# Gate logits in the attention stage: the tokens held in the array, the sixteen gate columns passing

## The reference, cut to what matters

```python
x = x + tanh(g_xattn) * attention(layernorm(x), ctx)      # 16 heads of 16
xn = layernorm(x)
logits = einsum('bld,ed->ble', xn, gate_weight)           # 8 experts
kth_val = sort(logits.reshape(-1))[expert_k - 1]
gates = logits * (logits >= kth_val)
h = gelu(einsum('bld,ehd->bleh', xn, w1) + b1)
y = einsum('bleh,edh->blde', h, w2) + b2
x = x + tanh(g_ffn) * einsum('blde,ble->bld', y, gates)
```

## Time and profile before

| | |
|---|---|
| three runs | 2002.65, 2004.87, 2005.2 us, median 2004.87 |
| profiled execution | 2004.73 us, of which the span between first and last instruction is 2002.9 |
| granted clock of TensorE, mean | 0.976 |
| busy: PE, PEld, DVE, ACT, POOL | 95%, 68%, 66%, 62%, 7% of the span |
| gate matmuls L887 | 32 |
| pick matmuls L894 | 64 |
| copies L1129, reads L1026 | 8 and 8 |

### The profile page before, as it was taken

One profiled execution on the slowest core, in us unless ns is written; L12 is line 12 of the kernel. 1 busy time (PEld: TensorE's weight loads), 2 busy tenths in 40 slices (PEclk: granted clock), 3 DMA queues, 4 the chain that ended last, 5 costly groups with the idle time before them and its releaser, 6 DMA issues.

```text
span 2002.9 us, 26039 instructions
## 1 busy us (share of the span) xinstructions
PE 1897.7 (95%) x8916; PEld 1357.2 (68%) x8916; DVE 1322.1 (66%) x2331; ACT 1242.3 (62%) x2081; POOL 146.7 (7%) x330
## 2 busy tenths in 40 slices
PE   7889999999968989999999999999999999999998
PEld 5743333333337867788788878878878887887886
DVE  6588888888725787565655665565665566656555
ACT  4447776767743323676676667667666666667664
POOL 4300011101112260000000000000000000000000
PEclk9979999999978999999999999999999999999999
DMA  6933323222110144333323333233422224232221
GB/s 240 329 118 86 83 71 83 71 74 70 49 53 24 74 176 184 122 143 114 106 84 108 148 118 110 85 106 119 149 101 94 106 98 161 97 108 84 106 105 53
DMA packets 97243, 220.81 MB, mean 110 GB/s; under 512 B 31314, under 2 KB 49492, under 8 KB 87892
## 3 DMA queue, kind: packets, MB, share of 16 engines
q1 hardware_dynamic: 97108, 219.12, 31.9%
HBM read 178.57 MB, written 40.24 MB: 109 GB/s over the span
## 4 chain that ended last, share of the span: by engine, by line
PE 61%; DVE 3%; ACT 2%; issue 2%; POOL 0%; ACTq 0%; DVEq 0%; POOLq 0%
PE ps_y L2140 29%; PE ps_h L2087 25%; PE ps_h L2047 4%; PE ps_y L2059 3%; ACT gelu L2294 1%; DVE w_pair L2520 1%; ACT w_pair L2264 1%; DVE early L2528 1%; DVE h_lo L2395 1%; DVE out_T_acc L2471 1%; ACT h_hi L2297 0%; DVE early L2483 0%; DVE h_hi L2391 0%; DVE gated L2464 0%; ACT copy L2304 0%
## 5 line engine op out<-in xcount | busy, mean ns | idle before, releaser
L2395 DVE TENSOR_TENSOR h_lo<-gelu,h_hi 128x512 fp32r<-128x512 f32 x512 | 355.4, 698 | 412.8 <-ACT h_hi L2297 411.7
L2087 PE MATMUL ps_h<-x_hi,w_pair 128*128 128x512 f32 x1568 | 567.3, 395 | 11.3 <-ACT gelu L2294 9.4
L2294 ACT ACTIVATE gelu<-early,b 128x512 f32<-128x512 f32 x336 | 243.2, 724 | 236.1 <-DVE early L2528 228.7
L2087 PEld LDWEIGHTS ps_h<-x_hi,w_pair 128*128 128x128 f32 x1568 | 294.5, 188 | 88.7 <-issue 13.4
L964 DVE TENSOR_REDUCE low<-ps_s 128x1 f32<-128x512 f32 x512 | 322.3, 684 | 35.2 <-PE ps_s L820 31.9
L2297 ACT ACTIVATE h_hi<-gelu 128x512 fp32r<-128x512 f32 x448 | 283.3, 632 | 42.0 <-ACT gelu L2294 0.7
L2087 PE MATMUL ps_h<-x_lo,w_pair 128*128 128x512 f32 x784 | 308.7, 394 | 0.0
L1096 ACT ACTIVATE probs_T<-ps_t 128x512 f32<-128x512 f32 x384 | 207.8, 600 | 105.3 <-PE ps_t L830 103.6
L2528 DVE TENSOR_TENSOR early<-ps_h,copy 128x512 f32<-128x512 f32 x336 | 230.7, 687 | 53.4 <-PE ps_h L2087 53.4
L820 PE MATMUL ps_s<-k_st,q_st 48*128 48x512 f32 x512 | 205.7, 480 | 3.2 <-SPq L736 2.0
L2140 PE MATMUL ps_y<-h_hi,w_hi 128*128 128x512 f32 x512 | 202.3, 395 | 3.5 <-DVE h_lo L2395 3.5
(11 more groups left out here) (252 smaller groups left out, 2614.3 us busy)
## 6 DMA issues: line engine op xcount, KB each, us to landing
x_hi<-blocks_scratch SPq DMA_DIRECT2D x28, 1024.0 KB, 5.1
x_lo<-blocks_scratch SPq DMA_DIRECT2D x28, 1024.0 KB, 8.8
x_hi<-blocks_scratch SPq DMA_DIRECT2D x28, 768.0 KB, 6.8
x_lo<-blocks_scratch SPq DMA_DIRECT2D x28, 768.0 KB, 10.2
gate<-gates_scratch SPq DMA_DIRECT2D x64, 256.0 KB, 3.3
q_st<-q_scratch SPq DMA_DIRECT2D x192, 64.0 KB, 2.4
k_st<-k_scratch SPq DMA_DIRECT2D x192, 64.0 KB, 2.4
k_scratch<-k_hl SPq DMA_DIRECT2D x8, 1024.0 KB, 3.9
```

The costliest lines, as they stand in the source:

```text
L2087: mm = pe.matmul(bank, w[wp], x[xp], start=start and n == 0, stop=n == 2, skip_group_check=not start)
L2294: act.activation(gelu[:, c % GELUS, :], src, ACT.Gelu_apprx_tanh, bias=b1[p][:, j:j + 1]).then_inc(gelu_done, 1)
L2395: dve.tensor_tensor(h_lo[:, j % RING, :], gelu[:, j % GELUS, :], h_hi[:, j % RING, :].bitcast(F32), ALU.subtract).then_inc(h_ready, 1)
```

## The change

The gate matmuls exchange their operands. For each of the 4 token tiles, 128 columns of `x_hi` or `x_lo` are held and the first 16 columns of `gw` pass: 4 tiles x 2 halves x 2 parts = 16 matmuls with 16 loads, which leave for each tile 128 tokens x 16 columns in the bank. VectorE adds leading and rest part with one reduction over pairs and writes `logits`. The unit `pick`, its matmuls, ScalarE's copy and the tile `logits_T` go. The reading on VectorE now belongs to the unit (3,1,1), and is taken in step (3,2).

```diff
-    (3, 1, 0): ("out", 0, 2), (3, 1, 1): ("logits", -1, 0), (3, 3, 0): ("pick", -1, 0),
+    (3, 1, 0): ("out", 0, 2), (3, 1, 1): ("logits", -1, 0),
...
-                for n, (x, k) in enumerate(parts):
-                    mm = pe.matmul(ps_m[:], gw[:, k, :], x[:, k, bass.ds(b * SEQ, SEQ)], start=(n == 0), stop=(n == len(parts) - 1))
+                for t in range(TT):
+                    out = ps_m[:, t * 2 * EXPERTS:(t + 1) * 2 * EXPERTS]
+                    for n, (x, k) in enumerate(parts):
+                        mm = pe.matmul(out, x[:, k, bass.ds(b * SEQ + t * P, P)], gw[:, k, 0:2 * EXPERTS],
+                                       start=(n == 0), stop=(n == len(parts) - 1))
                 return mm
 
-            def pick_logits(ps_m, b, i):
-
-                pe.wait_ge(taken["logits"], b + 1)
-                for t in range(TT):
-                    mm = pe.matmul(ps_m[:, t * EXPERTS:(t + 1) * EXPERTS], logits_T[:, t * P:(t + 1) * P], pick[:],
-                                   start=True, stop=True)
-                return mm
...
             def keep_logits(b, i):
-                dve.wait_ge(in_psum["pick"], b + 1)
-                dve.tensor_scalar(logits[:, :, bass.ds(b * TT, TT)], bank("pick", b, i)[:, 0:TT * EXPERTS].rearrange("p (t e) -> p e t", t=TT),
-                                  1.0, None, ALU.mult).then_inc(taken["pick"], 1)
+                dve.wait_ge(in_psum["logits"], b + 1)
+                both = bank("logits", b, i)[:, 0:TT * 2 * EXPERTS].rearrange("p (t w e) -> p t e w", t=TT, w=2)
+                dve.tensor_reduce(logits[:, :, bass.ds(b * TT, TT)].rearrange("p e t -> p t e"), both, AX_X, ALU.add).then_inc(taken["logits"], 1)
...
-            def take_logits(b, i):
-                act.wait_ge(in_psum["logits"], b + 1)
-                wait(act, in_psum["pick"], b)
-                act.activation(logits_T[:], bank("logits", b, i)[:], ACT.Copy).then_inc(taken["logits"], 1)
```

More of the change, by code:

```diff
@@ L562 @@
 UNITS_OF = {"low": GROUPS, "out": GROUPS, "rows": KT, "y": 2,
-            "x2T": KT, "xnT": KT, "logits": 1, "pick": 1}
+            "x2T": KT, "xnT": KT, "logits": 1}
 def exists(b):
@@ L638, in build_attend @@
         gw_raw = n_.sb("gw_raw", [P, KT, EXPERTS])
-        logits_T = n_.sb("logits_T", [P, SEQ])
         x_hi, x_lo, out_T, gw, pick, logits = (keep[name] for name in ("x_hi", "x_lo", "out_T", "gw", "pick", "logits"))
@@ L885, in gate_logits @@
                 parts = [(x, k) for k in range(KT) for x in (x_hi, x_lo)]
-                for n, (x, k) in enumerate(parts):
-                    mm = pe.matmul(ps_m[:], gw[:, k, :], x[:, k, bass.ds(b * SEQ, SEQ)], start=(n == 0), stop=(n == len(parts) - 1))
-                return mm
-            def pick_logits(ps_m, b, i):
-                pe.wait_ge(taken["logits"], b + 1)
                 for t in range(TT):
-                    mm = pe.matmul(ps_m[:, t * EXPERTS:(t + 1) * EXPERTS], logits_T[:, t * P:(t + 1) * P], pick[:],
-                                   start=True, stop=True)
+                    out = ps_m[:, t * 2 * EXPERTS:(t + 1) * 2 * EXPERTS]
+                    for n, (x, k) in enumerate(parts):
+                        mm = pe.matmul(out, x[:, k, bass.ds(b * SEQ + t * P, P)], gw[:, k, 0:2 * EXPERTS],
+                                       start=(n == 0), stop=(n == len(parts) - 1))
                 return mm
             write = {"low": turn_lows, "out": turn_out, "rows": turn_rows, "y": project_out,
-                     "x2T": turn_x2, "xnT": turn_xn, "logits": gate_logits, "pick": pick_logits}
+                     "x2T": turn_x2, "xnT": turn_xn, "logits": gate_logits}
             def shared(b, unit):
@@ L1044, in set_flag @@
                 dve.tensor_scalar(keep["clip_flag"][:], ps_t[0][:, 0:1], 3 * HEADS * TOKENS - 0.5, None, ALU.is_lt)
-            take = {"out": normalise, "y": add_residual, "xnT": split, "pick": keep_logits}
+            take = {"out": normalise, "y": add_residual, "xnT": split, "logits": keep_logits}
             def take_unit(b, at):
@@ L1136, in first_high @@
                     act.activation((w1_first, w2_first)[half][0][:, at, :], raw[:, at, :], ACT.Copy).then_inc(first_hi, 1)
-            take = {"low": take_lows, "rows": take_rows, "x2T": take_x2, "xnT": take_hi, "logits": take_logits}
+            take = {"low": take_lows, "rows": take_rows, "x2T": take_x2, "xnT": take_hi}
             def take_unit(b, at):
```

## The result

The changed kernel takes 2014.7 us (median of 18 runs, 2004.9 to 2018.2), the kernel before in the same jobs 2003.9 (18 runs, 1999.5 to 2006.9). The ratio is 1.0048, with an interval of 1.0037 to 1.0058: slower by 0.5%. The forecast was 2010.4, slower, by the clock. The profiled execution took 2011.79 us with a span of 2010.0, 2.9 under its median, so it shows less of the loss than a usual run has. Its mean granted clock was 0.967, which is also the median of the 18 executions; the 74 executions of the kernel before in the jobs of the experiments have a median of 0.976.

The account below looks back on a forecast made before the run. Batches were taken as bound by the order of TensorE's queue and its clock. From 2004.73 us: - 1.6 in seven batches, - 1.0 in the last, + 8.1 for the clock gave 2010.2, on the median 2010.4; range 2000.5 to 2015.8.

Parts of the forecast that it names:

- The pairs, 0.111 us each and 1.88 us in all: Step (3,1): 16 pairs of load and matmul replace four wide matmuls taking 1.12 us, + 0.76 us a batch on TensorE.
- would have halved it: Rival at step (3,1): fast weight loads make pairs cost half, two falls of the clock, 1994 us; chance 0.03.
- The pick's 0.99 us: Step (3,3): the pick's matmuls leave TensorE's queue, where it wasn't waiting, so the whole 0.99 us a batch comes off.
- a batch at full clock that isn't shorter than 56.0: Sign against the forecast, in the attention loop: full-clock batches were to take 55.8 us instead of 56.0.
- The copy and the read at nothing: ScalarE's 604 ns copy goes without gain; VectorE's read, 0.25 us, is hidden behind its 0.36 us wait for L820.
- The last batch, 1.0 us off: Same units alone at half clock before the barrier ending attention: last read at 598.0 instead of 598.97, 1.0 us off.
- The falls, five instead of two at 2.7 us each: Attention loop: the longer thin stretch at (3,1) makes the granted clock fall in five batches instead of two, + 8.1 us.
- the wide range: Whole program: 2000.5 to 2015.8 us, leaving out the faster rivals and the dearest end.
- the narrow one: Range of the forecast alone, for the whole program: 2007.5 to 2013 us.
- the end of the loop: Fall at 568, behind the seventh pick: counted unchanged, since TensorE soon has nothing to do there with either kernel.
- the second rival: Thin stretch at (3,3): falls go with the pick and none is left, 1996.9 us, faster; chance 0.10.
- read as one about idle gaps: First rival, at (3,1): loads follow without idle gap, so the clock does not follow; only work counts, 2002.3 us; chance 0.20.

Follow-up runs that it names:

- the column experiments: Changed kernel with 64 or 128 gate columns passing instead of 16: ratios 1.0013 and 0.9970; kernel before with 64 pick columns instead of 8: 0.9983.
- a narrow seventh gate alone: Changed kernel with 128 gate columns passing in all batches but one, the seventh gate unit keeping 16: 2000.3 us, ratio 0.9979.
- the wide pick: Kernel before, with 64 columns of the pick passing instead of 8, the further ones not read: 1999.2 us, ratio 0.9983.
- that with the copy: Changed kernel with 128 gate columns passing and a 128x512 copy put back on ScalarE at its old place: 1998.3 us, ratio 0.9969.

## Why the prediction was right

- **The pairs, 0.111 us each and 1.88 us in all.** Right to 0.01 us. The rule of the Trainium skill ("TensorE: Matmul & The Clock Gate", on fast weight loads) would have halved it; the loads of `x_hi` and `x_lo` do not go faster, 335.44 - 335.33 = 0.11.
- **The pick's 0.99 us.** It goes whole: from gate to gate at the full clock 55.77 us instead of 56.00, the forecast's 0.23. The forecast had named a batch at full clock that isn't shorter than 56.0 as a sign against it; the only such stretch, 172.0 to 228.0, is 56.0 long, but its counterpart before was 56.1, and the distance from gate to gate says that the sign didn't come.
- **The copy and the read at nothing.** Right, shown by putting both back. The read took 0.22 us (0.25 assumed).
- **The last batch, 1.0 us off.** It was 1.1.
- **The falls, five instead of two at 2.7 us each.** The mechanism is shown by the column experiments, in both kernels, and the place is right: the first four falls each start behind a gate and before step (3,3), the one at 337.8 for instance 0.6 us behind the L829 that ends the gate. The size is where the forecast was off. It put the clock at + 8.1 us: 13.5 for five falls behind narrow gates, less 5.4 for the pick's two. The runs have 15.6 less 3.4, + 12.2. So the forecast foresaw 5.5 us more in all, and 9.6 were measured by the ratio (10.8 between the medians); 2014.7 lies in the wide range and above the narrow one, which ended at 2013. The count of five was an estimate between none and seven, and that it came this near is in part luck.
- **Where the rest is.** In the profiled execution four falls, not five, stand in the first six batches, from 3.4 to 13.6 us long. Those batches take 346.0 us (172.0 to 518.0), and 335.4 (172.9 to 508.3) with 128 columns. With 0.3 for that kernel's dearer pairs, four falls cost 10.9 us, 2.7 each, as priced. What the forecast put at nothing is the end of the loop: from the last batch's start to the end of the last read it is 88.5 us (518.0 to 606.5) against 83.9 with 128 columns (508.3 to 592.2) and 84.7 before (514.3 to 599.0). Without the 1.1 us of work saved, that is 4.9 more than before. The fall there lasts 27.3 us instead of 13.7, but it begins at 563.0, 3 us ahead of the seventh gate (565.98). So that gate didn't start it. Whether the gate kept the clock low is open: a narrow seventh gate alone cost 2 us, and its profiled execution has 13.7 us at the lower clock.
- **"nothing but the pick preceded a fall so far"**, in the second rival, isn't so. The trace before also has the lower clock from 588.4 on, in the last batch's units behind the loop, and the fall at 568.0, counted as the pick's, has counterparts at 562.8 with 128 gate columns and at 566.4 with the wide pick. The argument used two falls only, and these were the pick's.
- With the measured terms, 2003.9 - 2.6 - 3.4 + 15.6 = 2013.5, beside 2014.7 measured.

The rule of the Trainium skill's page "TensorE: Matmul & The Clock Gate", section "Why this matters for your kernels", read as one about idle gaps, fails here: between 335.33 and 337.21 load followed load without a gap, and the clock fell at 337.8; with 128 columns between the same loads it didn't.

## What to carry to other kernels

Price a swap of held and passing operands twice: by the distance from load to load, and by what TensorE still streams in that time. A stretch of narrow matmuls can pay for itself in its own queue (2.6 us here) and lose several times that in the steps behind (15.6), at the lower clock; where the loads set the pace anyway, letting padding columns pass costs next to nothing (0.05 us in 16 pairs). 64 columns kept the clock behind the pick, but not behind the gates. The version with 128 columns is faster than both kernels (0.9970 of the one before, 0.9958 to 0.9981), and the same padding alone brought the kernel before to 0.9983.

## What the runs showed of the hardware

- A pair of a full load and a matmul of 16, 64 or 128 columns has the same pace, 0.11 us at 2.4 GHz; 16 pairs took 1.88 us with 16 columns and 1.93 with 128. At 1.2 GHz it was 0.21.
- Columns of zeros kept the clock up too: with 112 of 128 passing columns zero, the clock stayed full from 172.9 to 562.8 us.
- The same microsecond of narrow matmuls was nearly free at step (3,1) and cost 5 us more at (3,3) (0.9971 against 0.9997). The trace doesn't say why.
- Executions of one kernel differ with their mean clock: 2004.9 to 2018.2 us with 16 columns (18 runs, 0.974 to 0.965), 1997.7 to 2012.7 with 64 (12 runs, 0.979 to 0.967). The kernels with 128 columns spread too, 4.9 us in 6 runs of one and 12.7 in 10 runs of that with the copy (0.983 to 0.974), so the narrow gates are not the only source. One profile can't price such a change; here it lay 2.9 us from the median with 16 columns and 5.5 with 64.
